# Second expert layer of a mixture-of-experts block in three reduced-precision passes, with split operands

## The reference, cut to what matters

```python
probs = jax.nn.softmax(logits, axis=-1)                 # 16 experts
topk_w, topk_idx = jax.lax.top_k(probs, TOP_K)          # TOP_K = 8, then normalised to sum 1
for e in range(NUM_EXPERTS):                            # 8 of width 128, 8 of width 256
    h = jax.nn.gelu(xt @ w1[:, off:off + wd])           # first layer: 192 -> 128 or 256
    out = out + comb[:, e:e + 1] * (h @ w2[off:off + wd, :])   # second layer: back to 192
```

## Time and profile before

| | us |
|---|---|
| median of 3 runs (lowest, highest) | 736.73 (735.62, 738.35) |
| the profiled execution | 739.34 |
| its span in the trace | 737.6 |
| TensorE busy in the span | 680.3 (92%) |
| VectorE busy | 496.5 (67%) |
| ScalarE busy | 356.3 (48%) |
| GpSimd busy | 108.2 (15%) |
| mean granted clock of TensorE, share of full | 0.981 |

### The profile page before, as it was taken

How to read it: one execution, slowest core, us unless ns; L and a number is a source line. 1 busy time by engine, 2 the same in 40 slices (tenths; PEclk the granted TensorE clock), 3 DMA queues, 4 the chain that set the end, 5 groups by cost and what they waited for, 6 DMA issues and landing times.

```text
span 737.6 us, 30455 instructions
## 1 busy us (share of the span) xinstructions
PE 680.3 (92%) x13218; PEld 595.5 (81%) x13218; DVE 496.5 (67%) x1354; ACT 356.3 (48%) x921; POOL 108.2 (15%) x328
## 2 busy tenths in 40 slices
PE   5668999999999999999999999869999999999996
PEld 2457888788888888888888878748898898998986
DVE  5257778777878878877778877447456546646644
ACT  0125664655655655555555655534334344434432
POOL 0122123123123123223123211110000000000000
PEclk9969999999999999999999999979999999999999
DMA  8951111011011011111000000000000000000000
GB/s 311 300 182 60 61 48 44 33 44 48 33 60 33 32 60 32 32 61 32 32 4 5 4 4 4 4 1 2 1 1 21 0 0 21 0 0 21 0 0 22
DMA packets 12244, 30.48 MB, mean 41 GB/s; under 512 B 1120, under 2 KB 7392, under 8 KB 11616
## 3 DMA queue, kind: packets, MB, share of 16 engines
q1 hardware_dynamic: 12128, 28.73, 11.9%
HBM read 27.16 MB, written 1.57 MB: 39 GB/s over the span
## 4 chain that ended last, share of the span: by engine, by line
PE 76%; DVE 14%; ACT 5%; issue 3%; DMA 1%; POOL 1%; DVEq 0%; ACTq 0%; SPq 0%; POOLq 0%
PE ps L364 24%; PE ps L493 17%; PE ps L484 15%; PE ps L263 6%; DVE uu L734 3%; DVE sq L653 2%; PE ps L277 2%; PE ps L382 2%; PE ps L314 2%; DVE rf L741 2%; ACT qq L557 2%; PE ps L448 2%; PE ps L278 1%; ACT rr L561 1%; PE ps L375 1%
## 5 line engine op out<-in xcount | busy, mean ns | idle before, releaser
L884 DVE SCALAR_TENSOR_TENSOR acc<-ps,comb,acc 128x192 f32 x256 | 89.2, 411 | 90.3 <-PE ps L493 90.3
L493 PE MATMUL ps<-w_sb,work 128*128 128x192 f32 x768 | 139.9, 326 | 0.5 <-ACT work L633 0.3
L364 PE MATMUL ps<-rr 64*64 64x64 f32 x3840 | 131.4, 221 | 6.0 <-issue 3.3
L493 PEld LDWEIGHTS ps<-w_sb,work 128*128 128x128 f32 x768 | 129.2, 189 | 9.5 <-issue 1.7
L364 PEld LDWEIGHTS ps<-rr 64*64 64x64 f32 x3840 | 119.8, 136 | 18.7 <-ACT rr L561 10.6
L557 ACT ACTIVATE qq<-ps 128x384 f32<-128x384 f32 x192 | 92.3, 490 | 66.7 <-PE ps L364 64.7
L734 DVE SCALAR_TENSOR_TENSOR uu<-rr,qq 128x384 f32<-128x384 f32 x160 | 87.9, 559 | 50.8 <-ACT qq L557 44.6
L633 ACT ACTIVATE work<-ps 128x512 f32<-128x512 f32 x96 | 57.3, 597 | 133.6 <-PE ps L484 133.6
L561 ACT ACTIVATE rr<-ps 128x384 f32<-128x384 f32 x160 | 73.9, 490 | 80.6 <-PE ps L364 79.8
L364 PE MATMUL ps<-uu,qq 64*64 64x64 f32 x4608 | 96.6, 224 | 16.1 <-DVE uu L734 13.9
L364 PEld LDWEIGHTS ps<-uu,qq 64*64 64x64 f32 x4608 | 80.6, 134 | 33.9 <-DVE uu L734 30.6
(11 more groups left out here) (136 smaller groups left out, 1026.8 us busy)
## 6 DMA issues: line engine op xcount, KB each, us to landing
xtb<-xt_dram SPq DMA_DIRECT2D x16, 512.0 KB, 3.5
work<-x_dram SPq DMA_DIRECT2D x16, 512.0 KB, 3.4
wsh<-ws_dram SPq DMA_DIRECT2D x2, 1440.0 KB, 7.8
w_sb<-w_dram SPq DMA_DIRECT2D x1, 2304.0 KB, 26.3
w_a<-w_dram SPq DMA_DIRECT2D x1, 1536.0 KB, 13.2
w_b<-w_dram SPq DMA_DIRECT2D x2, 768.0 KB, 17.7
out_dram<-acc SPq DMA_DIRECT2D x4, 384.0 KB, 2.7
mult<-copies_dram SPq DMA_DIRECT2D x1, 512.0 KB, 12.8
```

The source lines that it names most:

```text
L364: last = pe.matmul(ps[z:z + 64, 2 * lane + i, 64 * j:64 * j + 64], lhs[r, lane, i, j, :], rhs[r, lane, i, j, :], start=True, stop=True)
L493: last = pe.matmul(ps[:, 2 + 2 * (e % 2) + j // 2, (j % 2) * DIM:(j % 2 + 1) * DIM], hid[:, c % 4, j * P:(j + 1) * P], w2_sb[:, c, :], sta ...
L884: last = dve.scalar_tensor_tensor(out=a, in0=ps[:, 2 + 2 * (e % 2) + j // 2, (j % 2) * DIM:(j % 2 + 1) * DIM].unsqueeze(1), scalar=comb[:, ...
```

## The change

The second layer is done in fp32r like the first, as three passes: high hidden times high weights, high hidden times low weights, low hidden times high weights. For that

- ScalarE also copies the chunk of `w2` into `w2h`, and evaluates the gelu twice, once into `hhi` (fp32r), once into `hid` (float32);
- VectorE takes the difference of the two into `hlo`, and no longer makes the low parts of `w1`;
- GpSimd makes all low weight parts, of `w1` (`wal`, half of `wb`) and of `w2` (`w2l`), three instructions a chunk, each waiting for the one before;
- all new buffers are three deep (`n % 3`, with `n` the running chunk of 96), and the accumulators of the first layer rotate over three banks;
- TensorE runs two chunks ahead: `up(n + 2)` stands in front of `down(n)`;
- `high_part(n + 3)` stands behind the gelus of chunk `n` and waits for `chunk_down`, which counts finished `down`s;
- the loops over the groups are written out, and the groups follow each other without a join.

```diff
+UPB = (0, 1, 6)
+        hhi, hlo = (sb(n, [P, 3, GT * P], F32R) for n in ("hhi", "hlo"))
+        w2h, w2l = (sb(n, [P, 3, DIM], F32R) for n in ("w2h", "w2l"))
 # GpSimd
-            for t in range(-3, NT + 1):
+            for t in range(-3, NT):
                 iteration(t)
+            def low_part(n):
+                c, k = n % HID, n % 3
+                pool.wait_ge(whi_ready, 2 * n + 2)
+                pool.tensor_tensor(wal[:, k, :], w1_a[:, c * P:(c + 1) * P], wah[:, k, :].bitcast(F32),
+                                   ALU.subtract).then_inc(wlo_ready, 1)
+                pool.wait_ge(wlo_ready, 2 * n + 1)
+                pool.tensor_tensor(wb[DB:P, k, :], w1_b[DB:P, c * P:(c + 1) * P], wb[DB:P, k, :].bitcast(F32),
+                                   ALU.subtract).then_inc(wlo_ready, 1)
+                pool.wait_ge(wlo_ready, 2 * n + 2)
+                pool.wait_ge(w2h_ready, n + 1)
+                pool.tensor_tensor(w2l[:, k, :], w2_sb[:, c, :], w2h[:, k, :].bitcast(F32),
+                                   ALU.subtract).then_inc(w2l_ready, 1)
+            pool.wait_ge(ffw_loaded, 64)
+            for n in range(3):
+                low_part(n)
+            iteration(NT)
+            for n in range(3, NT // GT * HID):
+                low_part(n)
 # TensorE
+            def up(g, c):
+                n = g * HID + c
+                pe.wait_ge(whi_ready, 2 * n + 2)
+                pe.wait_ge(wlo_ready, 2 * n + 2)
+                if n >= 3:
+                    pe.wait_ge(h_done, n - 2)
...
+            def down(g, c):
...
+                pe.wait_ge(hhi_ready, n + 1)
+                pe.wait_ge(w2h_ready, n + 1)
+                pe.wait_ge(hlo_ready, n + 1)
+                pe.wait_ge(w2l_ready, n + 1)
+                for j in range(GT):
...
+                    pe.matmul(o, hhi[:, k, tj], w2h[:, k, :], start=opens, stop=False, skip_group_check=True)
+                    pe.matmul(o, hhi[:, k, tj], w2l[:, k, :], start=False, stop=False, skip_group_check=True)
+                    last = pe.matmul(o, hlo[:, k, tj], w2h[:, k, :], start=False, stop=(c == FIRST[e] + WIDTH[e] - 1),
+                                     skip_group_check=True)
+                last.then_inc(chunk_down, 1)
+            up(0, 0)
+            up(0, 1)
+            for n, (g, c) in enumerate(chunks):
+                if n + 2 < len(chunks):
+                    up(*chunks[n + 2])
+                down(g, c)
 # ScalarE
+            def high_part(n):
+                if n >= 3:
+                    act.wait_ge(chunk_down, n - 2)
+                c = n % HID
                 for w, raw in ((wah, w1_a), (wb, w1_b)):
+                    act.activation(w[:, n % 3, :], raw[:, c * P:(c + 1) * P], ACT.Copy).then_inc(whi_ready, 1)
+                act.activation(w2h[:, n % 3, :], w2_sb[:, c, :], ACT.Copy).then_inc(w2h_ready, 1)
...
+            for n in range(NT // GT * HID):
+                act.wait_ge(up_done, n + 1)
+                act.activation(hhi[:, n % 3, :], ps[:, UPB[n % 3], :], ACT.Gelu_apprx_tanh).then_inc(hhi_ready, 1)
+                if n >= 4:
+                    act.wait_ge(hlo_ready, n - 3)
+                act.activation(hid[:, n % 4, :], ps[:, UPB[n % 3], :], ACT.Gelu_apprx_tanh).then_inc(h_done, 1)
+                if n + 3 < NT // GT * HID:
+                    high_part(n + 3)
 # VectorE
+            for n in range(NT // GT * HID):
+                g, c = divmod(n, HID)
+                e = EXPERT_OF[c]
+                if c == FIRST[e] and n > 0:
+                    add_expert((g * EXPERTS + e - 1) // EXPERTS, (e - 1) % EXPERTS)
+                dve.wait_ge(h_done, n + 1)
+                if n >= 3:
+                    dve.wait_ge(chunk_down, n - 2)
+                dve.tensor_tensor(hlo[:, n % 3, :], hid[:, n % 4, :], hhi[:, n % 3, :].bitcast(F32),
+                                  ALU.subtract).then_inc(hlo_ready, 1)
+            add_expert(NT // GT - 1, EXPERTS - 1)
```

More of the change, by code:

```diff
@@ L22 @@
 LC = LP * 64
+FIRST = [sum(WIDTH[:e]) for e in range(EXPERTS)]
+EXPERT_OF = [e for e in range(EXPERTS) for _ in range(WIDTH[e])]
+UPB = (0, 1, 6)
 def on(f):
@@ L184, in _ @@
                 tile_loads(t)
[L185 removed]
+            for g in range(NT // GT):
                 sp.wait_ge(expert_added, (g + 1) * EXPERTS + 2)
[L187 to L188 removed]
+                sp.dma_start(out[g * GT:(g + 1) * GT].rearrange("t p n -> p t n"),
+                             acc[:, g * GT:(g + 1) * GT, :]).then_inc(out_stored, 16)
             sp.wait_ge(out_stored, 16 * (NT // GT))
@@ L466, in _ @@
                 iteration(t)
-            pe.wait_ge(ffw_loaded, 64)
             pe.wait_ge(x2_saved, NT)
             pe.wait_ge(lexp, NT)
[L472 to L504, removed]
@@ new lines, in up @@
+            def up(g, c):
[4 more added lines that the diff above has]
+                    pe.wait_ge(h_done, n - 2)
+                tok4 = slice(g * GT * P, (g + 1) * GT * P)
+                k = n % 3
+                parts = ((wah, xhi, 0), (wah, xlo, 0), (wal, xhi, 0), (wb, xhi, 1), (wb, xlo, 1))
+                for m, (w, xs, half) in enumerate(parts):
+                    last = pe.matmul(ps[:, UPB[n % 3], :], w[:, k, :], xs[:, half, tok4], start=(m == 0), stop=(m == 4))
+                last.then_inc(up_done, 1)
@@ L507, in _ @@
+            chunks = [(g, c) for g in range(NT // GT) for c in range(HID)]
+            up(0, 0)
[4 more added lines that the diff above has]
+                down(g, c)
         @block.scalar
@@ L625, in _ @@
             high_part(1)
+            high_part(2)
             iteration(NT)
[L627 to L635, removed]
+            for n in range(NT // GT * HID):
[6 more added lines that the diff above has]
+                    high_part(n + 3)
         @block.vector
@@ L779, in router_weights, with add_expert @@
                 dve.tensor_scalar(comb[:, t, :], rt[:, 3, :], rst[:, 3:4], None, ALU.mult).then_inc(comb_ready, 1)
+            def add_expert(g, e):
+                dve.wait_ge(chunk_down, g * HID + FIRST[e] + WIDTH[e])
+                dve.wait_ge(expert_added, g * EXPERTS + e + 2)
+                for j in range(GT):
+                    a = acc[:, g * GT + j, :]
+                    last = dve.scalar_tensor_tensor(
+                        out=a, in0=ps[:, 2 + 2 * (e % 2) + j // 2, (j % 2) * DIM:(j % 2 + 1) * DIM],
+                        scalar=comb[:, g * GT + j, e:e + 1], in1=a, op0=ALU.mult, op1=ALU.add)
+                last.then_inc(expert_added, 1)
             def window(k, t):
```

41 lines of the change are left out of this document (12 added, 29 removed).

## The result

| | before | after |
|---|---|---|
| median of 6 runs (lowest, highest), us | 736.49 (735.34, 738.35) | 1101.15 (1098.4, 1101.89) |
| span of the profiled execution, us | 737.6 | 1096.5 |
| TensorE busy | 680.3 (92%) | 881.0 (80%) |
| mean granted clock of TensorE | 0.981 | 0.755 |

The changed kernel takes 1.494 times as long (95% interval 1.492 to 1.496): 365 us more. The time lies within the predicted range of 890 to 1160, but not where the forecast of 929 us put it, and outside the forecast's own 895 to 965; it is the first rival's case, the granted clock that falls.

The account below looks back on a forecast made before the run. TensorE bounds the kernel before; after the change it waits every chunk for new weights. 93 chunks of 4.52 us, 420.4 us, plus start and end gave 931.4 for this execution, forecast 929 us, own range 895 to 965, wider range 890 to 1160.

Parts of the forecast that it names:

- first rival: Expert stage: TensorE's granted clock falls to half, 2.4 us more a chunk, 1155 us throughout or some 1040; chance 0.20.
- The order of waits: Expert stage: after every down, TensorE waits 1.78 us for ScalarE's copies and GpSimd's low parts before up.
- The sum of one chunk: Expert stage: waits and matmuls from one down to the next add to 4.52 us, in place of 2.45.
- granted clock 1.0 in the stage: Expected sign in the profile after: TensorE keeps its full clock throughout the expert stage.
- Beside the path: Expert stage: gelus and hlo finish before down needs them, hlo at 2.6 us, with 0.4 to spare.
- The rule that the prediction weighed: Port sharing: hlo would wait for GpSimd's w2l, about 0.1 us a chunk, 10 us in all; not in the sum.
- VectorE's addition: An expert's first chunk: VectorE first adds the last expert, 1.39 us, done at 1.5, before the gelu.
- second rival: Second layer: a narrow fp32r matmul costs the float32 pair's 0.325 us, giving 1172 us; chance 0.10.
- lower bound of 0.086: Second layer: matmuls at the streaming pace of 0.086 us would take 0.29 off a chunk, or 27 us.
- third rival: Expert stage: GpSimd collides with VectorE on every chunk, up to 0.7 us each, giving 994 us; chance 0.12.
- fourth rival: Expert stage: the three-deep buffers cover the preparation, TensorE stays the bound, 736 or 707 us; chance 0.02.
- Ahead of the stage: Before the expert stage: GpSimd's three low parts delay the last tile's norm, so the stage begins 0.6 us late.

Follow-up runs that it names:

- ring4_swap: The changed kernel with weight buffers four deep in place of three and VectorE's hlo ahead of the expert addition: 736.02 us, ratio 1.0004 to the kernel before.
- f32wait: The changed kernel's order with the second layer left in float32, the copies still waiting for down(n-3): 916.97 us, ratio 1.245 to the kernel before.
- after_swap: The changed kernel with only VectorE's order changed, hlo ahead of the addition, buffers three deep: 1095.38 us, ratio 1.488 to the kernel before.
- ring4: The changed kernel with only its weight buffers made four deep in place of three: 830.57 us, ratio 1.129 to the kernel before.

## Why the prediction was right and where it was wrong

- **The order of waits: right.** `up` waits behind every `down` for copies and low parts, in the named places (92 of the 93 lie between 500 and 1090 us), 1.71 us each where 1.78 was summed. Freed of it, and with `hlo` ahead of the addition, the kernel loses nothing (ring4_swap); with it alone, it loses 181 us against the kernel before (f32wait, 917 - 736).
- **The sum of one chunk: near at full clock, with a wait missed.** 4.52 us was summed, 4.65 measured (500.64 to 505.29). By its parts: from the end of a `down` to `up` 1.71 us (1.78), `up` 1.24 (0.10 + 1.16), the second wait, for `hlo`, 0.14 (nothing), the starts of `down` 1.29 (1.23), its last matmul 0.27 (0.25). In the first part GpSimd's subtractions took 0.457 and 0.452 us (0.45 and 0.45), TensorE to ScalarE 0.04 (0.11), ScalarE to GpSimd 0.08 (0.14), GpSimd to TensorE 0.07 to 0.10 (0.05). With fillers holding the clock the whole kernel took 941 and 940 us for the forecast 929; the missed wait alone is 93 x 0.14 = 13 us.
- **The clock: wrong, and this is the step that failed.** The forecast rested on "granted clock 1.0 in the stage", with 0.20 for the first rival, and named a clock under 0.9 as a sign of being wrong. The stage ran at a mean of 0.58. That 1101 us still lies between 890 and 1160 is owed to that rival being inside the range, and not to the sum. The rival's price of 2.4 us a chunk was somewhat high, a round at the half clock taking 6.68 us for 4.65, so 2.03 more; the clock was up for about a sixth of the stage. The forecast looked only at TensorE's busy share, 61%. Its own rows had stretches of 47% and of 75% ahead of a fall, one on each side, and it set against them that others had stayed up. The runs show that the busy share of the records does not tell: f32wait stays up at 61%, the changed kernel falls with nearly the same wait and round (from 495 to 505 us it was at the full clock, busy 5.86 of 10 us, and fell there).
- **Beside the path: `hlo` was not hidden at the full clock.** The prediction had it ready at 2.6 us with 0.4 to spare. It ends 2.84 us after the `down` (498.93 to 501.77), since it takes 1.03 us beside `w2l` in place of 0.69, and 0.25 us more pass before TensorE starts, for which the sum had nothing. The rule that the prediction weighed and left out of the sum, 0.1 us a chunk and 10 us in all, was near what was measured, 0.14 and 13. The half clock hid this in the changed kernel: only 14 weight loads of `down` stand for 0.4 us from 500 to 1090 us, with three fillers all 92 do.
- **VectorE's addition: hidden, but only by the longer loop.** after_swap gains nothing clear. Once the wait for the copies went, the addition and `hlo` were a loop of their own of 3.98 us, worth 95 us (830.57 - 736.02), which the expectation of ring4 had missed.
- **Narrow fp32r matmuls (second rival): excluded.** They never cost 0.325 us. The lower bound of 0.086 is out as well while 128 columns are loaded. The Trainium skill (TensorE: Matmul & The Clock Gate, Weight-path perf modes) has the faster load only where the type is not float32, and does not name fp32r; the load records here show none for fp32r (191 ns in ring4, 189 for float32).
- **GpSimd against VectorE (third rival): wrong in its place.** The additions, with one input in the accumulators, delay no subtraction on GpSimd (0.457 us, 0.45 by interpolation). Two instructions that both read two inputs from on-chip memory do block each other: `hlo` 1.03 for 0.69 us, VectorE's `wb` 0.71 for 0.29, and GpSimd's `w2l` 0.92 for 0.59 when `hlo` had started first. This is the rule of the Trainium skill (SBUF — State Buffer, SBUF: two separate sides), and the traces agree on who collides with whom; the loser was done 0.13 to 0.14 us sooner than the rule's full wait and its full length would make it: `hlo` 0.55 us after `w2l` ended and not 0.69, `wb` 0.15 and not 0.29, `w2l` 0.46 after `hlo` and not 0.59.
- **Not slower (fourth rival)** needed the ring to cover the preparation. With one buffer more and VectorE's order turned it does, at 736 us, the number that rival had.
- **Ahead of the stage.** GpSimd's low parts put the last norm off by about 0.4 us (it started at 481.54, 0.50 us after its input was there at 481.04, before it was 0.09), with 0.6 summed. It is lost in the 3.8 us by which the stage started earlier; the execution profiled of before took 739.34 us for a median of 736.49, and had a stretch of half clock near 351 us that this one lacks. What the rest comes from is not shown.

## What to carry to other kernels

A ring of n buffers covers nothing if the user of a buffer stands directly behind the one that frees it; count how much of the bounding engine's work lies between the release and the next use, and do it for each loop that goes over another engine, since removing the longest bares the next. When the bounding engine is made to wait in every round, price it at both clock levels: here the same order of waits cost 205 us by itself and 160 us more by the clock. To tell the two apart, fill the waiting time with matmuls that nobody reads. A margin that hides one chain of work is worth checking at both levels too: at the half clock `hlo` was hidden, at the full clock it was not.

## What the runs showed of the hardware

- Three matmuls of 0.23 us put into each wait of 1.7 us held the granted clock at 1.00 where without them it was 0.56, and made the kernel 160 us faster.
- In the changed kernel the clock rose now and then for a few microseconds and fell again: it was 0.79 from 500 to 516 us, 0.50 from 520 to 530, 0.84 from 685 to 690.
- A series of fp32r matmuls that load 128 columns of weights each goes at 0.11 us a matmul, whether each streams 192 columns or two of three only 128; the time of a matmul's record (0.24 to 0.31 us) says nothing of that pace.
- Two instructions with two inputs each from on-chip memory, one on GpSimd and one on VectorE, cost whichever started second 0.33 to 0.42 us: `hlo` 1.03 us for 0.69, GpSimd's `w2l` 0.92 for 0.59, VectorE's `wb` 0.71 for 0.29.
